# The last pair's second convolution ahead of pair 6's gate, four pieces of the hand-over to the pages in another order, and the last 28 results closer

## The chip, the cores and the metric

The kernel runs on one core of a Trainium2 chip. The metric is the device time of one execution in microseconds; lower is better. A core has TensorE (PE), VectorE (DVE), ScalarE (ACT), GpSimd (POOL) and SyncE (SP), which run their own instruction streams and wait for one another by semaphores. DMA queues are issued from SP, ACT and POOL.

## What is computed

The input x has 16 images of 64 channels and 32x32 points. It goes through a binary convolution block and then, point by point (16384 tokens of 64 values), through a mixture of 16 experts of which each token takes 2:

```
x = x + conv_block(layernorm_over_channels(x))
    # pad, sign, 2x3 convolution with sign(w1), batch norm, relu,
    # pad, sign, 2x3 convolution with sign(w2), batch norm, + input, relu
t = tokens(x)                                  # 16384 x 64
n = layernorm(t)
p = softmax(n @ gate_w + gate_b); top 2 of 16, renormalised
t = t + sum over the 2 experts e of
        p_e * (silu(n @ w1[e]) * (n @ w2[e])) @ w3[e]
```

## The kernel before

**Stage 1, pairs.** Two images make a pair (128 partitions are 2 x 64 channels), so there are pairs 0 to 7. Each goes through centring, root of the variance, first and second convolution, residual, second centring, variance and root, turning of channels (`channels` puts the rows to be sent into `payload`), gate, choice of two experts, and *places*: counts and ranks on TensorE, and `slots` on VectorE, which computes where in a list of pages each token goes. POOL then sends the pair's 16 x 128 rows to that list in memory (`scatter`, L523, 16 indirect DMAs a pair). The steps are software-pipelined in a loop over t: in step t, TensorE works on pair t-1's convolutions, pair t-2's gate (with `b = t - 2`) and pair t-3's ranks. Each engine's program is written out by hand in its own order, and that order is what decides who waits.

**Stage 2, pages.** A page is 128 rows that share a set of four experts (a *line*). There are 147 pages in 37 groups of up to 4. SP loads a group's pages (L408, L409) once their rows are in memory; the order of the pages is computed after pair 3 (`order_pages`, `order_rows`). `order_rows` stands in VectorE's program behind a wait for pair 6's gate, since both use the bank `small`. TensorE turns the rows of a group (`turn_rows`, L857), ScalarE makes a float16 high part (`rows_high`) and VectorE the low part (`rows_low`, L1475). Per page TensorE computes 32 up products (L947, L948) with the four experts that the *roster* names; the offsets are read into TensorE's registers (`experts_of`), so the roster (8 short steps on VectorE, `roster_step`) must be there. ScalarE applies silu (L702), VectorE multiplies (`hide`, L1557), TensorE does the down products (L962), VectorE weighs and sums (L1568, L1578, L1583) and POOL gives each page's results back to memory with an indirect DMA (`give_back`, L511).

Pairs 0 to 3 are known before the first page is loaded; pairs 4 to 7 are still being placed while pages run. From group 10 on (`SOON` is 40 pages), SP loads pages only after the scatters of all eight pairs. Pair 5's places (`weights`, `slots`) are computed in the straight piece between the loop over pairs and the loop over pages. The second choice of pair 6 is made at page 1 and its slots at page 6; those of pair 7 at pages 6 and 11. POOL sends pair 7's rows alternately with the first 16 give-backs, and after that waits before each give-back of page n until `result_page(n)` pages have passed ScalarE (`silu_done`), and for the result itself. Pair 7's scatter order and some waits of POOL on other engines (`let_through`) space the sends: the fifth send of pair 4 asks for `gate_ready` of pair 6.

**The end.** Groups of the last pages are summed in twos (from page 132). When all give-backs have landed, SP loads the last pair's results, TensorE turns them, VectorE adds the input and ScalarE stores.

Of the kernel before, what the change touches and what calls it, by code (L numbers as in the profile page):

```python
# [6 lines left out]
ACT = mybir.ActivationFunctionType  # L7
# [8 lines left out]
P = 128  # L16
# [34 lines left out]
def metaformer_kernel(nc, x, w1, gamma1, beta1, mean1, var1, w2, gamma2, beta2, mean2, var2,  # L51
# [33 lines left out]
    with ExitStack() as ctx:  # L85
# [226 lines left out]
        def pages_of(g):  # L312
            return min(BY, PAGES - BY * g)
# [127 lines left out]
        def _(pool):  # L441
# [59 lines left out]
            def result_page(n):  # L501
                last = PAGES - 20
                return max(17 + 3 * n // 4, min(n, last) + 9 + 3 * max(n - last, 0) // 4)
# [33 lines left out]
        def _(act):  # L537
# [107 lines left out]
            def make_hi(m):  # L645
                act.wait_ge(weights_made, WM_SCALES)
                act.activation(up_w[m][:, :, :], up_raw[:, m, :, :], ACT.Copy, scale=scales[:, m:m + 1])\
                    .then_inc(hi_made, 1)

            act.wait_ge(dve_made, DM_ZEROS)  # L650
            for t in range(PAIRS + 2):
# [13 lines left out]
                if a < PAIRS:  # L665
                    for c in range(CH):
                        sign(c, a)
                    for c in range(CH):
                        square(c, a)
                    for c in range(CH):  # L670
                        copy(c, a)
                if 0 <= b < PAIRS:
                    channels(b)
# [15 lines left out]

            def rows_high(g):  # L690
                act.wait_ge(rows_turned, g + 1)
                if g >= 2:
                    act.wait_ge(up_ready, BY * (g - 1))
                width = pages_of(g) * P
                act.activation(xs_hi[g % 2][:, 0:width], rows_bank(g)[:, 0:width], ACT.Copy, scale=X_SCALE)\  # L695
                    .then_inc(xs_hi_ready, 1)

            def silu(n):
# [6 lines left out]
            act.preload_act_table_set("silu_and_others")  # L705
            rows_high(0)
            for n in range(PAGES):
# [13 lines left out]
        def _(pe):  # L721
# [142 lines left out]
            for t in range(PAIRS + 2):  # L864
# [23 lines left out]
                if t == PAIRS + 1:  # L888
                    turn_rows(0)
                if 0 <= b < PAIRS:  # L890
                    if b == 0:
                        pe.wait_ge(gate_in, 48)
                    gate(b)
                if 0 <= s < PAIRS:
                    for c in range(CH):
                        conv(1, c, s)
# [112 lines left out]
        def _(dve):  # L1009
# [529 lines left out]

            for k in range(8):  # L1540
                roster_step(0, k)
            weights(PAIRS - 3)
# [3 lines left out]
            newton_root(1, PAIRS - 1)  # L1546
            channels(PAIRS - 1)
            first_choice(PAIRS - 2)
            score(PAIRS - 1)
            rows_low(0)  # L1550

# [98 lines left out]
```

## Time and profile before

| what | value |
|---|---|
| three timed runs | 528.3, 532.3, 535.14 us; median 532.3 |
| profiled execution | 528.8 us, its span 526.8 us |
| mean granted clock of TensorE in it | 0.948 of 2.4 GHz |
| busy share of the span | PE 90%, DVE 75%, ACT 49%, POOL 54% |
| chain that ended last, by engine | PE 64%, DVE 14%, POOL 8%, issue 8%, ACT 3%, DMA 2% |

Times are in microseconds from the start of the span. An instruction's row gives its start, its length, and in brackets how long its engine had been idle before it and what ended that wait. Matmuls overlap, so that a row's length includes some of the next one's. Of a row that ends in xN, N instructions are merged.

### The profile page before, as it was taken

Reading aid. Unit: us, or ns where it says so; the run is one execution under the profiler, and the core shown is the slowest. Engines: PE = TensorE matmul, PEld = TensorE weight load, DVE = VectorE, ACT = ScalarE, POOL = GpSimd, SP = SyncE. Lnnn points to the kernel's source line nnn. Section 1 sums busy time; section 2 is a strip of 40 time slices with the busy share of each in tenths; the row PEclk is TensorE's granted clock in tenths of the full one; section 3 lists DMA queues with packets and bytes.
Section 4 is the critical chain, followed back from the end, with each engine's and each line's share of the span. In section 5 each row is a group of like instructions: output and inputs, shape, how many; then the busy total and the mean of one; then the engine's idle time right before and its main releaser. Section 6 shows DMA issues by size and latency. Waiting matters only on the chain.

```text
span 526.8 us, 15132 instructions
## 1 busy us (share of the span) xinstructions
PE 473.7 (90%) x4774; PEld 416.0 (79%) x4774; DVE 397.1 (75%) x917; ACT 257.0 (49%) x461; POOL 284.2 (54%) x378
## 2 busy tenths in 40 slices
PE   6889989898996858689999999999999999999983
PEld 6557667665774558679998999999999999999982
DVE  5457787988888779888766777777877778777783
ACT  4467788976884543224343443443434434344320
POOL 4000006877777777677777754445444454445652
PEclk9689899998998879789999999999999999999996
DMA  6981011020200343011213332232333524211034
GB/s 263 330 159 42 0 42 55 32 67 28 69 30 29 85 94 81 26 32 43 57 36 80 79 72 52 47 87 56 88 97 87 137 53 127 58 34 54 25 124 160
DMA packets 62664, 41.03 MB, mean 78 GB/s; under 512 B 50003, under 2 KB 54318, under 8 KB 62080
## 3 DMA queue, kind: packets, MB, share of 16 engines
q1 hardware_dynamic: 52208, 23.84, 19.7%
q0 software_dynamic: 8800, 8.94, 5.3%
q10 hardware_dynamic: 1584, 7.29, 3.4%
q8 instruction: 45, 0.74, 0.6%
q14 instruction: 27, 0.22, 0.1%
HBM read 21.46 MB, written 19.19 MB: 77 GB/s over the span
## 4 chain that ended last, share of the span: by engine, by line
PE 64%; DVE 14%; POOL 8%; issue 8%; ACT 3%; DMA 2%; SPq 1%; POOLq 0%; DVEq 0%; ACTq 0%
PE turn L962 21%; PE up L947 10%; PE up L948 10%; PE up L772 8%; POOL pages L523 5%; PE small L789 4%; POOL results L511 3%; PE small L818 3%; PE small L857 2%; PE up L747 2%; PE turn L801 1%; PE lines L969 1%; ACT rstd_wide L587 1%; DVE up_w L1166 1%; PE turn L862 1%
## 5 line engine op out<-in xcount | busy, mean ns | idle before, releaser
L511 POOL DMA_INDIRECT results<-result,page_in x147 | 146.7, 998 | 117.9 <-ACT xc L702 87.1
L523 POOL DMA_INDIRECT pages<-payload,slot_int x128 | 131.4, 1026 | 107.3 <-DVE slot_int L1376 69.5
L702 ACT ACTIVATE xc<-up,gate_unscale 128x512 f32<-128x512 f32 x147 | 101.2, 688 | 179.5 <-PE up L948 157.5
L947 PE MATMUL up<-xs_hi,up_w 128*128 128x128 f16 x1176 | 150.1, 221 | 7.6 <-DVE sq L1557 3.2
L948 PE MATMUL up<-xs_lo,up_w 128*128 128x128 f16 x1176 | 150.1, 221 | 0.0
L947 PEld LDWEIGHTS up<-xs_hi,up_w 128*128 x1176 | 124.1, 106 | 8.4 <-issue 8.3
L948 PEld LDWEIGHTS up<-xs_lo,up_w 128*128 x1176 | 116.6, 99 | 0.1
L1557 DVE SCALAR_TENSOR_TENSOR hidden<-up,hidden_scale,xc 128x512 f32<-128x512 f32 x74 | 55.5, 749 | 37.3 <-ACT xc L702 34.6
L962 PE MATMUL turn<-down_raw,sq 128*128 x584 | 80.2, 281 | 1.6 <-DVE branch L1568 0.4
L962 PE MATMUL turn<-down_raw,hidden 128*128 x592 | 78.1, 275 | 1.4 <-issue 0.4
L962 PEld LDWEIGHTS turn<-down_raw,sq 128*128 128x128 f32 x584 | 71.6, 193 | 9.2 <-issue 6.9
L962 PEld LDWEIGHTS turn<-down_raw,hidden 128*128 128x128 f32 x592 | 72.2, 193 | 6.3 <-issue 5.4
L1557 DVE SCALAR_TENSOR_TENSOR sq<-up,hidden_scale,xc 128x512 f32<-128x512 f32 x73 | 54.5, 747 | 21.2 <-ACT xc L702 19.5
L772 PE MATMUL up<-sign,conv_w 128*128 128x512 bf16 x192 | 53.2, 435 | 0.0
L772 PEld LDWEIGHTS up<-sign,conv_w 128*128 128x128 bf16 x192 | 21.1, 116 | 25.9 <-issue 11.1
L789 PE MATMUL small<-mean_col,sq 128*128 128x2 f32 x256 | 32.4, 257 | 6.1 <-ACT sq L613 3.5
L789 PEld LDWEIGHTS small<-mean_col,sq 128*128 128x128 f32 x256 | 31.8, 201 | 7.2 <-ACT sq L613 4.1
L1568 DVE TENSOR_TENSOR branch<-turn,page_in 128x512 f32<-128x512 f32 (+1 forms) x38 | 25.9, 683 | 6.2 <-PE turn L962 6.1
L1568 DVE TENSOR_TENSOR rstd_wide<-turn,page_in 128x512 f32<-128x512 f32 x36 | 24.8, 689 | 5.8 <-PE turn L962 5.7
L695 ACT ACTIVATE xs_hi<-small 128x512 f16<-128x512 f32 (+1 forms) x36 | 21.4, 594 | 9.7 <-PE small L857 9.6
L1475 DVE SCALAR_TENSOR_TENSOR xs_lo<-small,xs_hi 128x512 f16<-128x512 f32 (+1 forms) x36 | 24.3, 676 | 0.0
L857 PE MATMUL small<-ident,page_in 128*128 128x128 f32 x143 | 22.7, 283 | 0.8 <-DMA page_in<-pages 0.8
(238 smaller groups left out, 598.0 us busy)
## 6 DMA issues: line engine op xcount, KB each, us to landing
pages<-x ACTq DMA_DIRECT2D x4, 1332.0 KB, 10.8
page_in<-pages SPq DMA_DIRECT2D x147, 36.0 KB
page_in<-pages SPq DMA_DIRECT2D x147, 32.0 KB
x_in<-in_x SPq DMA_DIRECT2D x7, 512.0 KB, 3.5
out<-up_raw SPq DMA_DIRECT2D x5, 512.0 KB, 2.9
results<-result,page_in POOLq DMA_INDIRECT x147
up_raw<-in_L_ffn_w SPq DMA_DIRECT2D x4, 512.0 KB, 17.1
pages<-payload,slot_int POOLq DMA_INDIRECT x128, 2.2
```

What stands on the lines that cost most here:

```text
L511: pool.indirect_dma_start(out=results, out_offset=bass.IndirectOffsetOnAxis(ap=page_in[g % LOADS][:, k, D + AT_TOKEN:D + AT_TOKEN + 1].bit ...
L523: pool.indirect_dma_start(out=pages, out_offset=bass.IndirectOffsetOnAxis(ap=slot_int[q % PAYLOADS][:, t:t + 1], axis=0), in_=payload[q % ...
L702: act.activation(act_s[n % 2], up[n % 2][:, 0:CW], ACT.Silu, scale=gate_unscale[:, 0:1])\
L772: last = pe.matmul(cv[c], conv_w[:, which, t, :], image[:, c * ROWS + i:(c + 1) * ROWS + i, j:j + W], start=(t == 0), stop=(t == len(TAPS) ...
L789: last = pe.matmul(var_ps[n][:, 2 * j:2 * j + 2], sq[:, j * P:(j + 1) * P], mean_col[:, :], start=True, stop=True)
L857: last = pe.transpose(rows_bank(g)[:, k * P:(k + 1) * P], page_in[g % LOADS][:, k, 0:2 * D], ident[:, :])
L947: pe.matmul(target, own, xs_hi[g % 2][:, at], start=True, stop=False)
L948: last = pe.matmul(target, own, xs_lo[g % 2][:, at], start=False, stop=True)
L962: last = pe.matmul(target, hidden[n % RING][:, at], whole[:, bass.ds(e, D)], start=True, stop=True)
L1475: dve.scalar_tensor_tensor(out=xs_lo[g % 2][:, 0:width], in0=rows_bank(g)[:, 0:width], scalar=X_SCALE, in1=xs_hi[g % 2][:, 0:width], op0=A ...
L1557: dve.scalar_tensor_tensor(out=hidden[n % RING], in0=up[n % 2][:, CW:HW], scalar=hidden_scale[:, 0:1], in1=act_s[n % 2], op0=ALU.mult, op1 ...
L1568: dve.tensor_tensor(weighed[g % 2][:, k:k + count, :, :], down_pair(m)[:, 0:count, :, :], weights.unsqueeze(3).to_broadcast([P, count, PER ...
```

## The change

Five pieces of code move or change; the instructions are the same in number.

- TensorE, step t = 8 (`PAIRS`): `conv(1, c, 7)`, the second convolution of the last pair, stands before `gate(6)` instead of behind it. The product that turns the page order (L887) stays ahead of both.
- ScalarE, step t = 9: `rows_high(0)` stands before `channels(7)` instead of behind the loop and a table load.
- VectorE, between the loops: weights and slots of pair 5, root and channels of pair 7 and the low rows of group 0 come before the roster, and the score of pair 7 and the first choice of pair 6 come last, in that order.
- POOL: `last` in `result_page` is `PAGES - 28` instead of `PAGES - 20`; pages from 120 on are asked for earlier.

```diff
             def result_page(n):
-                last = PAGES - 20
+                last = PAGES - 28
                 return max(17 + 3 * n // 4, min(n, last) + 9 + 3 * max(n - last, 0) // 4)
...
+                if t == PAIRS + 1:
+                    rows_high(0)
                 if 0 <= b < PAIRS:
                     channels(b)
...
             act.preload_act_table_set("silu_and_others")
-            rows_high(0)
             for n in range(PAGES):
...
                 if t == PAIRS + 1:
                     turn_rows(0)
+                if t == PAIRS:
+                    for c in range(CH):
+                        conv(1, c, s)
                 if 0 <= b < PAIRS:
                     if b == 0:
                         pe.wait_ge(gate_in, 48)
                     gate(b)
-                if 0 <= s < PAIRS:
+                if 0 <= s < PAIRS - 1:
                     for c in range(CH):
                         conv(1, c, s)
...
-            for k in range(8):
-                roster_step(0, k)
             weights(PAIRS - 3)
             slots(PAIRS - 3)
             newton_slack(1, PAIRS - 1)
             newton_sum(1, PAIRS - 1)
             newton_root(1, PAIRS - 1)
             channels(PAIRS - 1)
+            rows_low(0)
+            for k in range(8):
+                roster_step(0, k)
+            score(PAIRS - 1)
             first_choice(PAIRS - 2)
-            score(PAIRS - 1)
-            rows_low(0)
```

TensorE in step t = 8, from the turning of pair 6's channels on (`page_at` is the page order, `gate_mat` the gate, `sign` with `conv_w` the convolution), before:

```order
L887 MATMUL small<-ident,page_at 2x128
L818 MATMUL small<-gate_mat,xc 128x32 x8
L772 MATMUL up<-sign,conv_w 128x512 x12
L827 MATMUL lines<-ident_b,chosen 128x128 x2
L835 MATMUL lines<-incident,chosen_t 128x160 x2
L758 MATMUL up<-x,center_mat 128x256 x4
L841 MATMUL lines<-line_hot,upper_b 128x340
```

and with the change:

```order
L888 MATMUL small<-ident,page_at 2x128
L773 MATMUL up<-sign,conv_w 128x512 x12
L819 MATMUL small<-gate_mat,xc 128x32 x8
L828 MATMUL lines<-ident_b,chosen 128x128 x2
L836 MATMUL lines<-incident,chosen_t 128x160 x2
L759 MATMUL up<-x,center_mat 128x256 x4
L842 MATMUL lines<-line_hot,upper_b 128x340
```

The twelve products of the convolution stand ahead of the eight of the gate; line numbers are one higher in the changed file.

VectorE between the loops, from pair 7's channels (`payload`) on: first choice of pair 6 (from `best` to `logits<-pick`), score of pair 7 (`logits<-small` and the next), low rows (`xs_lo`), first `hide`; before:

```order
L1227 TENSOR_TENSOR payload<-turn,rstd 128x8x64
L1258 TENSOR_REDUCE best<-logits 128x16
L1236 TENSOR_TENSOR match<-logits,best 128x256
L1239 TENSOR_TENSOR key<-match,first_rank 128x256
L1242 TENSOR_REDUCE best<-key 128x16
L1244 TENSOR_TENSOR pick<-key,best 128x256
L1265 SCALAR_TENSOR_TENSOR logits<-pick,logits 128x256
L1250 TENSOR_TENSOR logits<-small,rstd 128x256
L1253 TENSOR_TENSOR logits<-logits,gate_bias 128x256
L1475 SCALAR_TENSOR_TENSOR xs_lo<-up,xs_hi 128x512
```

and with the change, where the eight roster steps go from `reached` to the cast of `roster`:

```order
L1231 TENSOR_TENSOR payload<-turn,rstd 128x8x64
L1479 SCALAR_TENSOR_TENSOR xs_lo<-up,xs_hi 128x512
L1451 TENSOR_TENSOR reached<-page_at,opened 128x322
L1454 TENSOR_REDUCE total_reached<-reached 128x2
L1456 TENSOR_REDUCE pairs_behind<-reached 128x2
L1460 SCALAR_TENSOR_TENSOR line_of<-pairs_behind,total_reached 128x2
L1463 TENSOR_TENSOR on_page<-line_of,line_number 128x40
L1467 TENSOR_TENSOR expert_on_page<-on_page,expert_of 128x80 x2
L1471 TENSOR_REDUCE roster_f<-expert_on_page 128x8
L1473 CAST roster<-roster_f 128x8
L1254 TENSOR_TENSOR logits<-small,rstd 128x256
L1257 TENSOR_TENSOR logits<-logits,gate_bias 128x256
```

The low rows now follow channels at once, the roster follows them, and the score and the first choice, whose rows come next, stand behind it.

## Rows read from the trace of the kernel before

**Rows 1.** Waits of TensorE, 190 to 285 us: engine, line, releaser: us, times, longest.
```profile
PE small L857 <- DMA page_in<-pages: 0.8, 1, 0.8
```

**Rows 2.** Chain of waits: start us, us, what.
```profile
278.87 1.91 DMA page_in<-pages
```

**Rows 3.** Timeline of POOL: start us, us, engine, line, operation, tiles [idle before <-releaser].
```profile
173.98 0.96 POOL L523 DMA_INDIRECT pages<-payload,slot_int  x1 [0.30 <-issue]
...
212.29 0.96 POOL L523 DMA_INDIRECT pages<-payload,slot_int  x1 [2.11 <-DVE slot_int L1376]
```

**Rows 4.** Timeline of VectorE, 170 to 194 us.
```profile
170.47 0.28 DVE L1432 CAST order<-small 2x128 int32<-2x128 f32 x1 [0.83 <-PE small L818]
...
173.03 0.75 DVE L1190 SCALAR_TENSOR_TENSOR bn_sum<-up,bn,x_ln 128x512 f32<-128x512 f32 x1 [0.83 <-PE up L772]
...
175.34 0.75 DVE L1190 SCALAR_TENSOR_TENSOR bn_sum<-up,bn,x_ln 128x512 f32<-128x512 f32 x1 [1.56 <-PE up L772]
...
176.48 1.35 DVE L1197 TENSOR_TENSOR x<-x_in,bn_sum 128x512 f32<-128x512 f32 x2 [0.39 <-ACT bn_sum L604]
...
178.97 0.49 DVE L1447 TENSOR_TENSOR reached<-page_at,opened 128x322 f32<-128x322 f32 x1
...
181.94 0.17 DVE L1336 TENSOR_SCALAR rounded_up<-lines 128x20 f32<-128x20 f32 x1
...
185.98 0.19 DVE L1376 CAST slot_int<-slot 128x16 uint32<-128x16 f32 x1
...
187.37 0.41 DVE L1258 TENSOR_REDUCE best<-logits 128x16 f32<-128x256 f32 x1
...
190.79 0.68 DVE L1475 SCALAR_TENSOR_TENSOR xs_lo<-up,xs_hi 128x512 f16<-128x512 f32 x1
...
193.54 0.75 DVE L1557 SCALAR_TENSOR_TENSOR hidden<-up,hidden_scale,xc 128x512 f32<-128x512 f32 x1 [2.07 <-PE up L948]
```

**Rows 5.** Timeline of TensorE, 167 to 192 us.
```profile
167.40 0.27 PE L887 MATMUL small<-ident,page_at 128*2 128x128 f32 x1 [4.55 <-DVE slack L1213]
...
167.51 2.92 PE L818 MATMUL small<-gate_mat,xc 128*128 128x32 f32 x16
...
170.24 5.06 PE L772 MATMUL up<-sign,conv_w 128*128 128x512 bf16 x12
...
177.37 1.97 PE L758 MATMUL up<-x,center_mat 128*128 128x256 f32 x8 [1.17 <-DVE x L1197]
...
179.46 1.34 PE L845 MATMUL lines<-line_hot,ones_b 128*128 128x320 bf16 x16
...
183.35 0.60 PE L857 MATMUL up<-ident,page_in 128*128 128x128 f32 x4
...
186.52 1.97 PE L818 MATMUL small<-gate_mat,xc 128*128 128x32 f32 x16 [2.56 <-DVE slack L1213]
...
191.61 0.29 PE L947 MATMUL up<-xs_hi,up_w 128*128 128x128 f16 x1 [3.12 <-DVE xs_lo L1475]
```

**Rows 6.** Stretches: us, PE, PEld, DVE, ACT, POOL busy (instructions), clock, DMA share, GB/s.
```profile
171.00:172.50 1.50, 1.50 (x5) 0.58 (x4) 1.16 (x4) 0.00 (x0) 1.10 (x2) 0.50 0.08 27
...
192.00:193.50 1.50, 1.50 (x16) 1.50 (x14) 0.00 (x0) 0.69 (x1) 1.13 (x2) 0.50 0.41 87
```

**Rows 7.** Timeline of SP's DMA issues.
```profile
174.91 0.38 SPq L409 DMA_DIRECT2D page_in<-pages  x1
```

**Rows 8.** Timeline of ScalarE.
```profile
189.82 0.60 ACT L695 ACTIVATE xs_hi<-up 128x512 f16<-128x512 f32 x1
```

**Rows 9.** Timeline of POOL near the end.
```profile
510.98 0.98 POOL L511 DMA_INDIRECT results<-result,page_in  x1 [1.47 <-DVE result L1583]
```

**Rows 10.** Stretch 450 to 500 us, columns as in Rows 6.
```profile
450.00:500.00 50.00, 49.48 (x614) 47.13 (x614) 37.90 (x61) 20.11 (x31) 26.00 (x27) 1.00 0.17 43
```

**Rows 11.** VectorE's sum: 280 to 300 us, then 440 to 488; busy, mean ns, idle.
```profile
L1578 DVE TENSOR_TENSOR halves<-rstd_wide 128x512 f32<-128x512 f32 x1 | 0.7, 692 | 0.0
...
L1578 DVE TENSOR_TENSOR halves<-rstd_wide 128x512 f32<-128x512 f32 x3 | 2.1, 692 | 0.1
```

More of the change, by code:

```diff
@@ L648, in make_hi, with rows_high @@
                     .then_inc(hi_made, 1)
+            def rows_high(g):
+                act.wait_ge(rows_turned, g + 1)
+                if g >= 2:
+                    act.wait_ge(up_ready, BY * (g - 1))
+                width = pages_of(g) * P
+                act.activation(xs_hi[g % 2][:, 0:width], rows_bank(g)[:, 0:width], ACT.Copy, scale=X_SCALE)\
+                    .then_inc(xs_hi_ready, 1)
             act.wait_ge(dve_made, DM_ZEROS)
@@ L688, in _ @@
                     make_hi(0)
[L690 to L696, printed above, removed]
             def silu(n):
```

## The prediction

> **What bounds the kernel now.** I read the page's busy shares first: TensorE is busy 90% of the span, so in the long page stage the end is set by how many pages remain, and a change in front of that stage counts only if it moves the start of it or a stall inside it. The reader is to look for such stalls in TensorE's waits from 190 to 285 us: one wait there is for a page in memory, 0.8 us, at the turning of group 10 [rows 1]. Group 10 is the first group that may hold rows of the last pairs, so SP loads it only after all scatters of pair 7; the chain of waits shows that load at 278.87, 1.91 us long [rows 2]. The chain leads back over an unbroken row of POOL's DMAs (16 scatters of pair 6, then 16 of pair 7 with 16 give-backs between them) to 212.29, where POOL had stood idle for 2.11 us until pair 6's slots were cast [rows 3]. So two paths meet at 280 us, 0.8 us apart: TensorE's own pages, and the path over pair 6's slots and POOL. Whatever moves VectorE's work at the start of the page stage moves the second path one for one, since VectorE goes from its first product of `hide` (193.54, [rows 4]) to pair 6's slots almost without idling. That first `hide` is the number that I follow.
>
> **Part 1: the last convolution ahead of pair 6's gate, on TensorE.** The product that turns the page order stands ahead of both and waits 4.55 us for VectorE, until 167.40 [rows 5]. The convolution does not pass it, so it does not fill that gap; it only trades places with the gate. Gate: 167.51 to 170.24, 2.73 us. Convolution: 170.24 and 5.06 us as printed, or about 4.90 from start to start [rows 5]. Both ran at half clock (granted 0.50, the level of 1.2 GHz, [rows 6]) after that gap, which stays as it was, so I keep both lengths. Then the gate ends at about 167.51 + 4.90 + 2.73 = 175.14 where it ended at 170.24: 4.9 us later. Next I ask who waits for it. VectorE's next instruction in program order is the copy of the page order (170.47, 0.23 us behind the gate, [rows 4]); it waits for the gate, and the add-ins of the convolution's result are queued behind it. From that copy to the point where VectorE was free for the add-ins took 173.03 - 0.83 - 170.47 = 1.73 us. After the change: copy at 175.37, free at 177.10, add-ins at 177.10 and 177.76, residual 1.14 us behind the second one (176.48 - 175.34) at 178.90. It was at 176.48, so **+2.4 us**: the convolution's result lies ready and nobody takes it.
>
> Centring of pair 7 (177.37) and the ranks of pair 5, whose last product ends at 179.46 + 1.34 = 180.80 [rows 5], stand behind that residual on TensorE and go with it: ranks ready at 183.2. Others behind the gate: the copy of the order also releases SP's page loads. Group 0's last load was issued at 174.91 [rows 7]; 4.9 later and with 1.91 us to landing it is there at 181.7, and group 0 is turned at 183.35 + 2.4 = 185.75 [rows 5], so about 4 us of cover remain. POOL's fifth scatter of pair 4 (173.98, [rows 3]) asks for the same gate and stalls about 1.4 us; the 2.11 us of idleness before pair 6 hides that.
>
> **Part 2: the order of VectorE's last steps ahead of the pages.** Before: roster, weights and slots of pair 5, root and channels of pair 7, first choice of pair 6, score of pair 7, low rows. The roster with the weights took 181.94 - 178.97 = 2.97 us [rows 4], of it about 0.4 for the two weight instructions (my estimate from their size), so the roster 2.6. Slots 5 are now free of it and wait for the ranks: they start at 183.2 in place of 181.94, **+1.3 us**, where without part 1 they could start at about 181.0, 0.9 earlier. From there: slots cast 185.98 + 1.3 = 187.3; root and channels 187.37 - 185.98 = 1.39, to 188.7; the low rows now follow at once, 0.6 of VectorE's time, to 189.3 (before: 190.79). The high rows that they need took 0.60 us on ScalarE at 189.82 [rows 8], behind channels; now they stand ahead of them and run from about 186.4, so they are hidden, at no cost. The eight roster steps end at 189.3 + 2.6 = 191.9. TensorE waits for rows and roster, and reads the four offsets of its first page only then; before, that reading lay in the wait of 3.12 us for the low rows. I have no row for its length; between 0.2 and 0.9 us it puts the first page product at 192.1 to 192.8 (it was 191.61, [rows 5]). Score and first choice, 190.79 - 187.37 = 3.42 us [rows 4], now lie behind the roster: VectorE is free at 191.9 + 3.4 = 195.3. The product that `hide` needs is 193.54 - 191.61 = 1.93 us behind the first page product, at 194.0 to 194.7, so VectorE is the later one whatever the reading costs. First `hide` at 195.3 where it was 193.54: **+1.8 us**. The 2.07 us that VectorE idled there are used up by the 3.4 us put in, which is why taking work off the way to the low rows brings nothing.
>
> **Part 3: the last 28 results closer.** `result_page` holds a give-back until a later page has passed ScalarE, and is now closer for pages 120 to about 138. At the end POOL is not behind: it idled 1.47 us for VectorE's result at 510.98 [rows 9], and the last five follow one another whatever went before. **0 us.**
>
> Sum: 528.8 us (the profiled execution, span 526.8) + 1.8 + 0 = 530.6. That execution is at the low end of what was seen; the mean of it and the three timed runs (528.3, 532.3, 535.14) is 531.1, their median alone 532.3. I add the 1.8 to 531.1: **532.9 us**, 0.3% slower, which no measurement of this kernel can tell from nothing: about 2% is what one can tell.
>
> **Rivals.**
> 1. *The trade costs nothing on the way to pair 5's slots* (chance 0.20). If the convolution's early result reaches the residual in the old time, say since the pair runs faster than the half clock of [rows 6] once the wide products come first, the ranks are ready at 181.0, the first `hide` comes at 193.0 (0.9 + 3.4 as above against 193.54), and the sum is -0.5: 530.6 from the mean. Against it: VectorE's queue cannot reach the add-ins before the gate.
> 2. *The clock* (0.20, slower side). After the wait of 3.12 us the first pages still ran at 0.50 at 193.5 [rows 6], so from 191.61 at least 1.9 us of products went at half clock, a loss of 1.0. The slow stretch at the convolution covered about 7.8 us of products (167.51 to 170.24 + 5.06, [rows 5]). If the second one falls as fully on page products, it costs 3.9 in place of 1.0; with half of that 2.9 hidden behind VectorE, which sets the pace there, that is +1.4 on top of 1.8: 534.3.
> 3. *Group 0 arrives late* (0.05, slower). Decides when its loads take over 4 us longer than 1.91; each us beyond delays all pages. At 3 us beyond, 535.9.
> 4. *POOL closer to VectorE's sums* (0.03, slower). If a give-back and a sum exclude each other, seven sums of two instructions meet a POOL instruction of 0.98 us [rows 9]: up to 13.7 us, of which VectorE's idleness there (50 - 37.9 us in 50, [rows 10]) takes 9.7 over 40 us; +4.0, 536.9. Against it: the same sum lasts 692 ns where POOL works without a break and 692 ns where it works half the time [rows 11].
>
> [...]
>
> The forecast itself has 0.50; 0.02 is left for what I do not see.
>
> **Numbers.** The cases reach from 530.6 to 536.9 around a mean of 531.1, while single runs of the same kernel lay 2.8 below and 4.0 above that mean. The low end is case 1 in a low run (528.3 - 0.5 = 527.8, rounded to 528.0), the high end the clock case at 534.3 with most of the upper spread: 537.5. All cases but the last lie inside 2%: faster 0.02, same 0.95, slower 0.03.
>
> **What the new profile would show.** The gate of pair 6 behind the twelve wide products, ending near 175; the copy of the order right behind it and both add-ins with no idle time; the residual near 178.9; slots of pair 5 cast near 187.3; xs_lo of group 0 ahead of the roster, near 188.7; the first `hide` near 195.3 with no idle time before it; POOL idle for about 2.4 us before pair 6 (2.11 + 1.8 - 1.4); TensorE's wait at group 10 still near 0.8. I am wrong if the residual is not later than 176.5, if the first `hide` comes by 193.5, or if POOL's way to group 10 opens before pair 6's slots.

## The result, and the profile after

| | before | with the change |
|---|---|---|
| 20 runs each, median | 530.91 us (526.18 to 539.82) | 535.79 us (531.81 to 543.11) |
| ratio of after to before, 95% interval | | **1.0088 [1.0056, 1.0119]** |
| profiled execution | 528.8 us, span 526.8 | span 535.2 us |
| granted clock, mean | 0.948 | 0.921 |

The change makes the kernel slower by about 4.7 us (0.88%). I had forecast 0.3%, 532.9 us in a range of 528.0 to 537.5: the sign and the places were right, the size was a little over a third of the measured one. The interval does not hold 1, though I had written that such a difference could not be told from nothing. The same kernel against itself (r1 below) gave 1.0041 [0.9979, 1.0104].

The spans of the two profiles differ by 8.4 us, and that is not the cost of the change. The product that turns the page order, ahead of which TensorE's instructions are the same, starts at 167.40 us before [rows 5] and at 171.78 after. These 4.4 us come from where stretches of half clock fall in stage 1 (last section). So I count everything from that product, in every profile, and call it the *anchor*. (The ratios leave out single runs more than 1.5% above the fastest of the same kernel; the profiled executions of e1, e10 and r1 were such runs, and r1 shows that up to pair 6's slots the piece behind the anchor is none the longer for it.)

TensorE with the change (timeline: start us, length, engine, line, operation, tiles, idle time before and its releaser):

```profile
171.78 0.37 PE L888 MATMUL small<-ident,page_at 128*2 128x128 f32 x1 [4.25 <-DVE slack L1217]
...
171.94 5.32 PE L773 MATMUL up<-sign,conv_w 128*128 128x512 bf16 x12
...
177.06 1.97 PE L819 MATMUL small<-gate_mat,xc 128*128 128x32 f32 x16
...
183.08 3.75 PE L759 MATMUL up<-x,center_mat 128*128 128x256 f32 x8 [3.15 <-DVE x L1201]
...
187.19 1.51 PE L846 MATMUL lines<-line_hot,ones_b 128*128 128x320 bf16 x16
...
198.44 0.28 PE L951 MATMUL up<-xs_hi,up_w 128*128 128x128 f16 x1 [2.00 <-DVE roster L1473]
```

The convolution is ahead of the gate and took 5.1 us from start to start, the gate ends near 178.9, and centring (L759) finds nobody's residual: TensorE idles 3.15 us. To be seen behind it: centring takes 3.75 us for the eight products that took 1.97 before [rows 5], and the ranks come late in turn. The granted clock in 183 to 188 was 0.55, as the stretches of the same profile show (columns as in Rows 6):

```profile
183.00:188.00 5.00, 4.92 (x16) 3.60 (x17) 2.04 (x7) 3.12 (x6) 3.98 (x4) 0.55 0.46 96
...
205.00:207.00 2.00, 0.99 (x15) 0.85 (x16) 2.00 (x4) 0.59 (x3) 1.59 (x2) 1.00 0.52 108
...
209.00:211.00 2.00, 2.00 (x20) 2.00 (x21) 1.93 (x5) 0.64 (x1) 1.65 (x2) 0.50 0.29 75
```

The other two rows matter further on: at 209 to 211, in the middle of the first pages, it is at 0.50 again. VectorE, same profile:

```profile
179.07 0.28 DVE L1436 CAST order<-small 2x128 int32<-2x128 f32 x1 [5.05 <-PE small L819]
...
180.71 1.40 DVE L1194 SCALAR_TENSOR_TENSOR bn_sum<-up,bn,x_ln 128x512 f32<-128x512 f32 x2
...
182.24 1.35 DVE L1201 TENSOR_TENSOR x<-x_in,bn_sum 128x512 f32<-128x512 f32 x2
...
188.74 0.18 DVE L1340 TENSOR_SCALAR rounded_up<-lines 128x20 f32<-128x20 f32 x1 [3.49 <-PE lines L846]
...
192.92 0.31 DVE L1380 CAST slot_int<-slot 128x16 uint32<-128x16 f32 x1
...
194.38 0.68 DVE L1479 SCALAR_TENSOR_TENSOR xs_lo<-up,xs_hi 128x512 f16<-128x512 f32 x1
...
197.44 0.17 DVE L1473 CAST roster<-roster_f 128x8 int32<-128x8 f32 x1
...
201.06 0.74 DVE L1561 SCALAR_TENSOR_TENSOR hidden<-up,hidden_scale,xc 128x512 f32<-128x512 f32 x1
...
219.96 0.17 DVE L1380 CAST slot_int<-slot 128x16 uint32<-128x16 f32 x1
```

Order copy behind 5.05 us of idleness, add-ins and residual in one unbroken row at 182.24, which is 10.46 us behind the anchor (before 9.08); slots of pair 5 start 16.96 behind it (14.54) and wait 3.49 us for the ranks; low rows ahead of the roster; first `hide` at 201.06, 29.28 behind the anchor (26.14 before), without idling, as forecast. And the slots of pair 6 are cast at 219.96, which is 48.18 behind the anchor. Before, that row was

```profile
211.31 0.17 DVE L1376 CAST slot_int<-slot 128x16 uint32<-128x16 f32 x1
```

43.91 behind it. So 4.27 us are lost up to there: 3.14 ahead of the first `hide`, 1.13 behind it. From the slots of pair 6 to the end it is 315.24 us after and 315.49 before, the same within 0.3. What POOL waited for ahead of pair 6's first scatter:

```profile
220.94 0.96 POOL L523 DMA_INDIRECT pages<-payload,slot_int  x1 [5.79 <-DVE slot_int L1380]
```

It idled 5.79 us before pair 6's first scatter, where it had idled 2.11 in the kernel before [rows 3] (3.28 and 3.39 in two other profiles with this piece unchanged, e3 and r1). TensorE's wait at group 10, forecast near 0.8 us, was

```profile
289.04 0.66 PE L858 MATMUL small<-ident,page_in 128*128 128x128 f32 x4 [0.18 <-DMA page_in<-pages]
```

0.18 us, because TensorE's own pages had become as late as the load: it turned group 9 at 104.33 us behind the anchor before and at 108.72 after. Group 0 was turned without a wait for its pages.

### The profile page after: what moved, and what is told of

The parts are those of the page before. It is cut to its first block, busy times and chain, and to the rows that moved or that the text cites. A ratio compares the mean times of both kernels' runs of the same rounds, so it can differ in the third digit from the quotient of the medians.

```text
span 535.2 us, 15132 instructions
## 1 busy us (share of the span) xinstructions
PE 483.1 (90%) x4774; PEld 421.7 (79%) x4774; DVE 397.7 (74%) x917; ACT 257.4 (48%) x461; POOL 281.2 (53%) x378
## 3 DMA queue, kind: packets, MB, share of 16 engines
q10 hardware_dynamic: 1584, 7.29, 3.4%
## 4 chain that ended last, share of the span: by engine, by line
PE 69%; DVE 8%; POOL 8%; issue 7%; ACT 4%; DMA 2%; SPq 1%; ACTq 0%; POOLq 0%; DVEq 0%
PE turn L966 21%; PE up L773 10%; PE up L951 10%; PE up L952 9%; PE small L790 5%; POOL pages L523 5%; POOL results L511 3%; PE small L858 2%; PE small L819 2%; PE up L748 2%; PE turn L802 2%; PE up L759 1%; PE lines L846 1%; PE lines L973 1%; PE turn L813 1%
## 5 line engine op out<-in xcount | busy, mean ns | idle before, releaser
L523 POOL DMA_INDIRECT pages<-payload,slot_int x128 | 129.2, 1010 | 118.8 <-DVE slot_int L1380 76.9
L773 PE MATMUL up<-sign,conv_w 128*128 128x512 bf16 x192 | 57.2, 459 | 0.0
```

What stands on the lines that cost most here:

```text
L523: pool.indirect_dma_start(out=pages, out_offset=bass.IndirectOffsetOnAxis(ap=slot_int[q % PAYLOADS][:, t:t + 1], axis=0), in_=payload[q % ...
L773: last = pe.matmul(cv[c], conv_w[:, which, t, :], image[:, c * ROWS + i:(c + 1) * ROWS + i, j:j + W], start=(t == 0), stop=(t == len(TAPS) ...
```

## The experiments

All profiles in one table, in us. "Anchor" is the start of the product that turns the page order; the other columns are counted from it. "To the end" is the span less the anchor.

| kernel | anchor | residual of 7 | first hide | slots of 6 cast | to the end | time against before |
|---|---|---|---|---|---|---|
| before | 167.40 | 9.08 | 26.14 | 43.91 | 359.4 | |
| before, again (r1) | 175.61 | 8.84 | 25.99 | 43.76 | 360.2 | 1.0041 [0.9979, 1.0104] |
| the change | 171.78 | 10.46 | 29.28 | 48.18 | 363.4 | 1.0088 [1.0056, 1.0119] |
| the change, again (r2) | 174.92 | 9.26 | 27.40 | 47.83 | 364.1 | 1.0115 [1.0032, 1.0198] |
| e1 order of VectorE and tail only | 178.33 | 8.91 | 25.34 | 45.17 | 361.2 | 1.0040 [1.0000, 1.0081] |
| e2 convolution only | 167.64 | 9.47 | 27.49 | 45.12 | 362.0 | 1.0061 [1.0013, 1.0108] |
| e3 tail only | 171.43 | 9.08 | 26.21 | 43.88 | 359.4 | 0.9986 [0.9933, 1.0040] |
| e4 convolution in the gap | 171.66 | 5.34 | 24.30 | 41.99 | 358.5 | 0.9977 [0.9930, 1.0024] |
| e4, again (r4) | 174.12 | 5.36 | 23.10 | 40.78 | 357.5 | 0.9969 [0.9920, 1.0018] |
| e6 change, add-ins first | 176.71 | 7.23 | 24.48 | 42.10 | 359.4 | 1.0146 [1.0062, 1.0229] |
| e7 change, wait filled | 167.93 | 9.47 | 25.89 | 45.64 | 361.7 | 1.0134 [1.0067, 1.0201] |
| e9 gap, choice in the wait | 174.80 | 5.36 | 23.65 | 41.33 | 357.8 | 535.44 against 532.49 us, no ratio |
| e10 change, pages filled | 176.94 | 9.27 | 27.36 | 45.01 | 361.9 | 1.0008 [0.9952, 1.0063] |
| r3 gap, add-ins first | 173.92 | 3.73 | 22.56 | 40.23 | 357.4 | 0.9968 [0.9916, 1.0019] |

How steady the column is: the three profiles in which nothing of this piece is changed (before, r1, e3) give 43.91, 43.76 and 43.88 us to the slots of pair 6 and 359.4, 360.2 and 359.4 to the end, though their anchors lie 8 us apart. A single run's time spreads by 13 us; the pieces behind the anchor are what tells kernels apart here. Two other kernels were profiled twice and agree less well: the change differs from its repeat by 0.35 us at the slots and 0.7 at the end, e4 from its repeat by 1.21 and 1.0. A difference of about 1 us between single profiles is therefore not safe.

**e1, the order of VectorE and the tail alone** (convolution back behind the gate).

```diff
-                if t == PAIRS:
-                    for c in range(CH):
-                        conv(1, c, s)
                 if 0 <= b < PAIRS:
...
-                if 0 <= s < PAIRS - 1:
+                if 0 <= s < PAIRS:
```

> The changed kernel with the last convolution back behind pair 6's gate: VectorE's and ScalarE's new order and the closer last results stay. I measure from the product that turns the page order on TensorE to VectorE's first product of hide: 26.1 us before (167.40 to 193.54), 29.3 us with the whole change (171.78 to 201.06). Theory A (the convolution's place costs, because VectorE's add-ins stand in its queue behind the wait for the gate): 25.6 us, half a microsecond better than before, time 0.998 to 1.001 of before. Theory B (the new order on VectorE costs: 3.4 us of score and first choice now between roster and first hide): about 28 us and time 1.005 or more.

First hide 25.34 behind the anchor: theory A to within 0.3 us, B falls for the part ahead of the pages. But the slots of pair 6 are 45.17 behind it, not 43.3, and the time is 1.0040. The loss lies behind the first `hide`, where neither theory had it. TensorE's anchor and VectorE's rows in e1:

```profile
178.33 0.37 PE L888 MATMUL small<-ident,page_at 128*2 128x128 f32 x1 [3.61 <-DVE slack L1214]
```

```profile
203.67 0.74 DVE L1558 SCALAR_TENSOR_TENSOR hidden<-up,hidden_scale,xc 128x512 f32<-128x512 f32 x1
...
216.19 0.69 DVE L1569 TENSOR_TENSOR branch<-turn,page_in 128x512 f32<-128x512 f32 x1 [1.23 <-PE turn L963]
...
223.50 0.17 DVE L1377 CAST slot_int<-slot 128x16 uint32<-128x16 f32 x1
```

From first `hide` to slots it takes 19.83 us where it took 17.77 before. Inside it `weigh` (second row) waits 1.23 us for TensorE, which it did not in the kernel before. This was my first surprise, and e10 is made for it.

**e2, the convolution alone.**

```diff
+                if t == PAIRS:
+                    for c in range(CH):
+                        conv(1, c, s)
                 if 0 <= b < PAIRS:
...
-                if 0 <= s < PAIRS:
+                if 0 <= s < PAIRS - 1:
```

> The kernel before with nothing but the last convolution ahead of pair 6's gate (behind the product that turns the page order). Theory A: the residual of pair 7 starts about 2.4 us later counted from that product (9.1 us behind it before, 11.5 now), TensorE then idles about 3 us for it, and the first hide comes at 28.5 us or more from the product; time 1.004 to 1.010. Theory B: as before, 26.1 us, time within 0.2%.

```profile
167.64 0.27 PE L887 MATMUL small<-ident,page_at 128*2 128x128 f32 x1 [4.54 <-DVE slack L1216]
...
177.95 3.75 PE L758 MATMUL up<-x,center_mat 128*128 128x256 f32 x8 [3.15 <-DVE x L1200]
```

Theory A in direction: TensorE's wait for the residual is 3.15 us (1.17 before) and centring is at half rate. The sizes are smaller than expected: residual at 9.47 in place of 11.5, since in this profile the granted clock fell later, so that the convolution ran in 4.28 us and the gate in about 1.8. First hide 1.35 later, slots of pair 6 1.21 later, 2.3 us to the end (mean of the three profiles with this piece unchanged: 359.7), ratio 1.0061. Theory B's "as before" falls. From 22 to 114 us behind the anchor the mean granted clock is 0.87 (0.90 and 0.91 in the two profiles of before), and TensorE turns group 10 without a wait for its pages, 115.68 us behind the anchor (113.42 and 114.29): here TensorE's own pages are the later path.

**e3, the last 28 results closer, alone.**

```diff
-                last = PAGES - 20
+                last = PAGES - 28
```

> The kernel before with nothing but the last 28 results closer. Theory A (POOL is not behind at the end, it waits for VectorE's results): the last five give-backs follow as before, the end unchanged, time 0.998 to 1.002. Theory C (POOL beside VectorE's sums slows them, one port pair held by one of the two): the sums of 128x512 in the last 40 us take longer than 692 ns and the time is 1.003 or more.

```profile
507.09 0.98 POOL L511 DMA_INDIRECT results<-result,page_in  x1 [1.60 <-DVE result L1583]
...
514.98 0.98 POOL L511 DMA_INDIRECT results<-result,page_in  x1 [1.50 <-DVE result L1583]
```

POOL waits for VectorE's result 1.60 and 1.50 us before the last give-backs, as it waited 1.47 in [rows 9]; 0.9986 and 359.4 us to the end. Nothing, as forecast. The sums in its last stretch:

```profile
L1578 DVE TENSOR_TENSOR halves<-branch 128x512 f32<-128x512 f32 x2 | 1.4, 692 | 0.1
```

692 ns, no more than in [rows 11]: C falls.

**e4, the convolution in the gap**, one place further forward than in the change.

```diff
                 if t == PAIRS:
+                    for c in range(CH):
+                        conv(1, c, s)
                     pe.wait_ge(order_link, 18)
...
-                if 0 <= s < PAIRS:
+                if 0 <= s < PAIRS - 1:
```

> The kernel before with the last convolution one place further forward than in the change, ahead of the product that turns the page order, so that it falls into TensorE's wait of 4.5 us. Theory A: it runs at full clock in 2.7 us, the gate keeps its time or ends earlier, the add-ins find their result ready behind an order copy that is not late, the residual starts 2 to 4 us earlier, and the first hide comes at 22.5 to 24 us from the product that turns the order; time 0.992 to 0.997 of before. Theory B says nothing here; a theory by which the residual is not what paces this piece (D: the root of pair 7 or the page loads do) expects 26 us and no change.

```profile
171.66 0.27 PE L889 MATMUL small<-ident,page_at 128*2 128x128 f32 x1 [0.76 <-DVE slack L1215]
...
177.83 3.75 PE L758 MATMUL up<-x,center_mat 128*128 128x256 f32 x8 [3.16 <-DVE x L1199]
```

The wait ahead of the anchor is 0.76 us in place of 4.55 and the residual comes at 5.34, 3.7 earlier; theory D falls, the residual paces this piece. First hide 24.30, 1.8 us better. Half of the early residual is lost in the hand-over: TensorE still idles 3.16 us for it, now because the gate ends earlier too, and centring again runs at half rate. To the end 358.5 us; ratio 0.9977, whose interval holds 1.

**e6, the add-ins ahead of the wait for the gate**, on the changed kernel.

```diff
                     if t == PAIRS:
+                        for c in range(CH):
+                            conv2(c, s)
+                        for c in range(CH):
+                            residual(c, s)
                         dve.wait_ge(gate_ready, b + 1)
                         order_rows()
...
-                if 0 <= s < PAIRS:
+                if 0 <= s < PAIRS - 1:
                     for c in range(CH):
                         conv2(c, s)
```

> The changed kernel, and on VectorE the add-ins and residual of pair 7 now stand ahead of the wait for pair 6's gate. Theory A (the queue behind that wait is what made the traded convolution a loss): the residual starts at about 7 us behind the product that turns the page order (10.5 with the change, 9.1 before), although the order copy stays at about 7.3 or later; TensorE's wait for the residual shrinks from 3.15 us to under 1. The first hide then comes at 26 us or a little less in place of 29.3, and the time falls to about before, ratio 1.000 to 1.005. A theory by which the late order copy (page loads) makes the loss expects 29 us still.

```profile
176.71 0.37 PE L888 MATMUL small<-ident,page_at 128*2 128x128 f32 x1 [3.67 <-DVE slack L1217]
...
184.78 1.96 PE L759 MATMUL up<-x,center_mat 128*128 128x256 f32 x8 [1.11 <-DVE x L1201]
...
192.79 0.66 PE L858 MATMUL up<-ident,page_in 128*128 128x128 f32 x4 [1.10 <-DMA page_in<-pages]
```

This is the test of the step by which I had forecast a loss, and it holds: with the convolution still traded, residual at 7.23 in place of 10.46 or 9.26, TensorE's wait 1.11 in place of 3.15, centring at full rate, first hide at 24.48 (27.40 and 29.28), although the order copy is later than ever (8.45). The late copy now costs something else: TensorE waits 1.10 us for group 0's pages (third row). It turns them 3.4 us earlier than with the change (16.08 against 19.47 behind the anchor) and the copy is 1.2 later, which uses up the 4 us of cover that I had estimated. To the end it is 359.4, as before the change. The timed ratio, 1.0146 from four runs, says the opposite. The profile is of the run of 537.84 us, whose length lies ahead of the anchor (176.71); the other three runs have no profile. So e6 shows the effect of the queue in the piece, and not in the time.

**e7, TensorE's wait filled**, on the changed kernel; the extra products go to a bank that centring overwrites.

```diff
+                if q == PAIRS - 1 and c == 0:
+                    for k in range(14):
+                        pe.matmul(cen[0], conv_w[:, 1, 0, :], sign2[:, 0:ROWS, 0:W], start=True, stop=True)
                 pe.wait_ge(x2_ready, CH * q + c + 1)
```

> The changed kernel with 14 extra 128x512 products (their result is overwritten) on TensorE where it waits 3.15 us for pair 7's residual: it is no longer idle there. Theory A with the clock (the idle time let the granted clock fall to 1.2 GHz, so that centring and the first ranks ran at half rate): centring takes 1.97 us in place of 3.75, pair 5's slots start 1.3 to 1.8 us earlier (15.3 in place of 16.96 behind the product that turns the order), the first hide at 27.5 to 28 in place of 29.3, the time 0.2 to 0.4% better than the changed kernel. Without a role of the clock: everything at its old place or later by what the extra products exceed the wait.

```profile
167.93 0.37 PE L891 MATMUL small<-ident,page_at 128*2 128x128 f32 x1 [3.52 <-DVE slack L1220]
...
174.92 3.19 PE L758 MATMUL up<-sign,conv_w 128*128 128x512 bf16 x14
...
178.14 1.99 PE L762 MATMUL up<-x,center_mat 128*128 128x256 f32 x8
```

Centring 1.99 us in place of 3.75 or 3.51: the half rate came of the idle time. The other profiles agree: behind waits of 3.15 to 3.33 us (both of the change, e2, e4 and its repeat, e9, e10) and of 1.70 (r3) centring ran at half rate, behind waits of 1.11 to 1.17 (before, r1, e1, e3, e6) at full rate. The slots of pair 5 start at 13.71 (16.96 and 15.11), the first hide is at 25.89, more than expected. To the end 361.7, 2 us less than the changed kernel. Again the time of four runs (1.0134), of which one is profiled, does not show it.

**e10, the early pages filled**, on the changed kernel.

```diff
+                if n == 3:
+                    pe.wait_ge(channels_ready[0], PAIRS)
+                    for k in range(5):
+                        pe.matmul(turn[0][:, :], conv_w[:, 1, 0, :], sign2[:, 0:ROWS, 0:W], start=True, stop=True)
                 if n in TURN:
                     turn_chosen(TURN[n])
+                if n == 3:
+                    for k in range(5):
+                        pe.matmul(turn[0][:, :], conv_w[:, 1, 0, :], sign2[:, 0:ROWS, 0:W], start=True, stop=True)
```

> The changed kernel with twice five extra 128x512 products (their result is overwritten) at page 3, around the turning of pair 6's choice, where TensorE waits 1.43 and 1.24 us for VectorE. Theory A with the clock (VectorE 1.2 us behind TensorE at the first hide, TensorE idles more there, the clock falls and pages 4 to 5 run at half rate): the half-clock stretch 6 to 9 us behind the first hide is gone, and slots of pair 6 are cast 17.8 us behind the first hide in place of 18.9. If the stretch has nothing to do with that idle time, 18.9 stays, or 19 to 20 by the extra products.

Its first hide is at 204.30. The stretches 4 to 10 us behind it:

```profile
208.00:210.00 2.00, 2.00 (x14) 1.05 (x13) 2.00 (x5) 0.49 (x2) 1.39 (x3) 1.00 0.42 93
...
210.00:212.00 2.00, 1.98 (x28) 1.81 (x25) 1.90 (x5) 0.69 (x1) 1.67 (x2) 1.00 0.32 66
...
212.00:214.00 2.00, 2.00 (x30) 2.00 (x27) 1.93 (x5) 1.17 (x2) 1.42 (x2) 1.00 0.34 80
```

No half clock, where the changed kernel had 0.50 in 209 to 211, 8 us behind its first `hide`. First `hide` to slots of pair 6: 17.65 us, where the changed kernel took 18.90 and 20.43 and e1 19.83. It starts from the same first `hide` as r2 (27.36 and 27.40), and has 2.8 us less at the slots. But e6 has no such stretch either (17.62 us), with nothing filled, so one profile of e10 does not show that the filling did it. To the end 361.9, time 1.0008.

**e9, gap, and the first choice in VectorE's wait for the ranks.**

```diff
+                    for c in range(CH):
+                        conv(1, c, s)
                     pe.wait_ge(order_link, 18)
...
             for k in range(8):
                 roster_step(0, k)
+            first_choice(PAIRS - 2)
             weights(PAIRS - 3)
...
             channels(PAIRS - 1)
-            first_choice(PAIRS - 2)
+            rows_low(0)
             score(PAIRS - 1)
-            rows_low(0)
```

(and `rows_high(0)` ahead of `channels(7)`, as in the change)

> A version meant to beat both: the last convolution ahead of the product that turns the page order; roster first as in the kernel before; first choice of pair 6 behind the roster, where VectorE waits for the ranks of pair 5; then weights and slots 5, root and channels 7, low rows at once (high rows early on ScalarE), score of pair 7 last; results as before. Theory A: residual at 5.3 us, slots of pair 5 at about 13.2, low rows at 19, first page product at 19.7, first hide at 21.6 us (24.3 with the convolution in the gap alone, 26.1 before) with VectorE idle ahead of it, so that no page product waits for VectorE and no half-clock stretch falls on pages 2 to 4; slots of pair 6 at 39 to 40 (43.9 before). Time 0.990 to 0.995 of before, if pair 6's slots and POOL still set the way to group 10; 0.997 if TensorE's early pages already filled the time.

Residual 5.36 and low rows at 19.15 as expected, but the first hide at 23.65, 2 us later: pair 7's gate ran at half rate (3.62 us), and so did the first pages, at 0.50 from 7 us ahead of the first `hide` to 3 behind it. 357.8 us to the end; four runs, with no ratio. It is not shown to beat the plain e4 (358.5 and 357.5).

**r1 and r2, both kernels again.**

> The kernel before, unchanged, for a second profile. In the profiles so far the product that turns the page order starts anywhere from 167.4 to 178.3 us though nothing ahead of it differs; steps of stage 1 take 11.5 or 14.8 us as half-clock stretches fall. Theory A: the piece from that product to pair 6's slots is 43.9 us here too, within 1.5, wherever the product lies; ratio 1.000 within its interval. If the piece itself swings by 3 us or more, the 4.3 us that it grew with the change is not shown by one pair of profiles.

```profile
175.61 0.37 PE L887 MATMUL small<-ident,page_at 128*2 128x128 f32 x1 [3.69 <-DVE slack L1213]
```

```profile
219.37 0.18 DVE L1376 CAST slot_int<-slot 128x16 uint32<-128x16 f32 x1
```

219.37 - 175.61 = 43.76: the piece is as long as in the first profile, with the anchor 8.2 us later.

> The changed kernel, unchanged, for a second profile. Theory A: the piece from the product that turns the page order to pair 6's slots is 2 to 4.5 us longer than in the kernel before (46 to 48.5), the residual 9.3 to 10.5 us behind the product, TensorE idle about 3.15 us for it; ratio 1.005 to 1.010.

```profile
174.92 0.37 PE L888 MATMUL small<-ident,page_at 128*2 128x128 f32 x1 [3.68 <-DVE slack L1217]
...
185.02 3.51 PE L759 MATMUL up<-x,center_mat 128*128 128x256 f32 x8 [3.15 <-DVE x L1201]
```

```profile
202.32 0.74 DVE L1561 SCALAR_TENSOR_TENSOR hidden<-up,hidden_scale,xc 128x512 f32<-128x512 f32 x1
...
222.75 0.17 DVE L1380 CAST slot_int<-slot 128x16 uint32<-128x16 f32 x1
```

47.83 us to the slots. The change costs 4.27 in one pair of profiles and 4.07 in the other, though it falls differently: 1.41 ahead of the first `hide` and 2.66 behind it here, 3.14 and 1.13 in the first. In r2 centring took 3.51 but ranks ran at full rate; in exchange 0.50 fell on the pages.

**r3 and r4, versions that might beat both.** r4 is e4 again; r3 is e4 with the add-ins first, as in e6.

> The last convolution ahead of the product that turns the page order, and VectorE's add-ins and residual of pair 7 ahead of the wait for pair 6's gate; all else as in the kernel before. Theory A: residual 3.5 us behind the product (5.3 with the convolution in the gap alone), order copy at 5 to 6, no wait of TensorE for the residual above 1.5 us, first hide at 22.5 to 23.5 (24.3), slots of pair 6 at 40.3 to 41.2 (42.0; 43.9 before). POOL then is the one that comes last before pair 6's scatter, so that little of it reaches the end: time 0.994 to 0.999 of before.

```profile
173.92 0.27 PE L889 MATMUL small<-ident,page_at 128*2 128x128 f32 x1 [0.21 <-DVE slack L1215]
...
178.49 3.75 PE L758 MATMUL up<-x,center_mat 128*128 128x256 f32 x8 [1.70 <-DVE x L1199]
```

Residual 3.73, order copy 5.00, first hide 22.56, slots of pair 6 40.23, all as expected; TensorE's wait 1.70, and centring all the same at half rate.

> The convolution in the gap alone, once more, as its 0.9977 had an interval that holds 1. Theory A: first hide at 24.3 and slots of pair 6 at 42.0 us behind the product that turns the order, 1.9 us ahead of the kernel before; time 0.995 to 0.999, better than both kernels.

First hide 23.10 and slots 40.78, a little better than e4. Both are 3.1 to 3.6 us ahead of before (43.85) at the slots of pair 6, and 2.2 to 2.3 at the end: 357.4 and 357.5 against 359.7. The medians on one chip were 529.49 and 530.35 against 534.5 for before and 536.98 for the changed kernel. Against before the intervals still hold 1 ([0.9916, 1.0019] and [0.9920, 1.0018]), so that they are faster than before is likely and not settled. They are faster than the changed kernel, whose interval on that chip begins at 1.0032.

## Why the prediction was right, and where its size was off

That 535.8 us lies in the range is partly luck and proves little: I had widened the range by the spread of single runs, so that it would have held any shift of the mean of 531.1 from -3.1 to +6.4 us. What the sum says of each step is the test.

**The traded convolution is a loss, because VectorE's add-ins stand behind the wait for the gate.** Right. The gate ended 4.9 us later by my sum, the order copy came 4.2 later (7.29 against 3.07), the add-ins followed without a pause, and e6, which changes nothing but that queue, takes the loss back up to the first `hide` and, in its profile, to the end. The size was too high: the sum gave +2.4 for the residual; against the mean of the two profiles of before (8.96) it was +1.5 in the first profile and +0.3 in r2: the residual was 3.2 us behind the order copy and not 3.5, and in r2 the order copy itself came at 6.09, the convolution having run partly at full clock. I had kept half clock for both, but behind the convolution the gate took 1.8 us and not 2.73. So the condition of my rival 1, a pair that runs faster than half clock, came true in part, and in r2 nearly in full.

**What follows the residual goes with it, at unchanged lengths.** Wrong in size, the other way. I moved centring and ranks by 2.4 us and kept their 1.97 and 1.34 us. In fact TensorE's wait grew from 1.17 to 3.15 us and what came next ran at half clock: centring alone 3.75. Slots 5 went from 14.54 to 16.96, +2.4 in place of the +1.3 of my sum; in r2 they came at 15.11, +0.7 against r1 (14.38). e7 shows it: with the wait filled centring is 1.99. That the mean of +2.4 and +0.7 is near my +1.3 is luck: a residual sized too high and a centring sized too low partly cancel.

**VectorE sets the first hide, +1.8.** Right in kind: VectorE came to it without idling, with 3.5 us of score and first choice put in behind the roster. Measured +3.1 and +1.4, of which the slots of pair 5 bring +2.4 and +0.7; the new order itself adds 0.7 both times, where my sum had 0.5. The reading of the offsets, for which I had no row, took 0.8 us (roster cast until 197.61, first page product at 198.44). That taking work off the way to the low rows brings only half a microsecond was right as well: e1 has its first `hide` at 25.34, 0.7 ahead of the mean of before, where I had said 0.5.

**From there to pair 6's slots nothing changes.** This step failed: "VectorE goes from its first product of `hide` to pair 6's slots almost without idling". With the new order it idles, +1.1 and +2.7 us. A second half-clock stretch of TensorE falls on the first pages, and VectorE waits for its products and for ScalarE's silu of them (0.62 and 0.57 us in the first profile, 1.65 and 0.73 in r2). That is near my rival 2, the clock on the slower side, to which I gave 0.20 and +1.4 us: the kind fits, only that it is a second stretch and not the first one moved, and the price was 1.1, 2.7, 2.1 (e1) and 2.0 us (e7).

The stretch goes with the new order of VectorE. It is there in four of the five profiles that have this order and nothing put in at page 3 (the change twice, e1, e7; not e6), in none of the seven with the old order (before, r1, e2, e3, e4 and its repeat, r3), nor in e9 or e10. What sets it off is open. It is not simply that TensorE idles longer there. Its waits in the 7 us behind the first `hide`, in r2 (with the stretch; first `hide` 202.32) and in r1 (without; 201.60):

```profile
207.26 0.23 PE L951 MATMUL up<-xs_hi,up_w 128*128 128x128 f16 x1 [1.24 <-DVE hidden L1561]
...
208.87 1.96 PE L966 MATMUL turn<-down_raw,hidden 128*128 x8 [0.49 <-DVE sq L1561]
```

```profile
205.03 0.28 PE L827 MATMUL lines<-ident_b,chosen 128*128 128x128 bf16 x2 [0.75 <-DVE chosen L1290]
...
206.56 0.23 PE L947 MATMUL up<-xs_hi,up_w 128*128 128x128 f16 x1 [1.24 <-DVE hidden L1557]
...
208.01 1.10 PE L962 MATMUL turn<-down_raw,hidden 128*128 x8 [0.34 <-DVE sq L1557]
```

These are 1.7 us with the stretch and 2.3 without it.

**The tail: 0.** Right (e3, 359.4 us to the end).

**The sum.** Counted to the end, e1 alone costs 1.5 us (361.2 against 359.7) and e2 alone 2.3, together 3.8, and the whole change 3.7 and 4.4. At the slots of pair 6 they do not add up: 1.3 and 1.3 alone, 4.3 and 4.0 together. With single profiles that differ by up to 1 us from a repeat, I take from this only that each part costs something. My sum had -0.5 for the first and so 2.3 for the second. The first is the term that was off: +1.5 in place of -0.5, lost from the first `hide` to the slots. The second came out as forecast at the end, but again not by my path: 1.2 shows at the slots, and the rest lies on TensorE's own pages, which in e2 are the later path to group 10.

**The rest of the path** I had as pair 6's slots, POOL, group 10, with TensorE's own pages 0.8 us ahead. What was lost up to the slots was still lost at the end (315.24 against 315.49 us), but both paths were late by the same: TensorE's wait at group 10 was 0.18 us, and 1.68 in r2, against 0.79 and none in the two profiles of before. These runs do not tell which of the two carried the loss. POOL's idleness was forecast at 2.4 (2.11 + 1.8 - 1.4 is in fact 2.5) and was 5.79, by the later slots. In the other direction it is not one to one: r3 wins 3.6 us up to the slots and 2.3 at the end. Rival 3, group 0 too late, did not come with the change; rival 4 fell with e3.

## What to carry to other kernels

Bringing work forward on one engine pays only if the engine that takes its result can reach it: look at what the consumer is waiting for in its own program, and if that is the thing just pushed back, the trade is a loss. A wait of 3 us on TensorE is not only its own length: see at what clock the products behind it run. Where single runs spread by more than the effect, count from an event ahead of which nothing differs, to one behind the change; here that piece agreed to 0.15 us in three profiles while the times spread by 13. Profile each kernel twice all the same: two others differed from their own repeats by 0.35 and 1.21 us.

## What the runs showed of the hardware that was not expected

The anchor lay anywhere from 167.40 to 178.33 us although the engines run the same instructions ahead of it (but for the convolution itself in e4, r3, r4 and e9). The difference is in the granted clock. Stretch 75 to 80 us before, and then with the change:

```profile
75.00:80.00 5.00, 4.59 (x30) 3.16 (x31) 4.86 (x24) 4.33 (x8) 0.00 (x0) 1.00 0.01 2
```

```profile
75.00:80.00 5.00, 5.00 (x17) 2.92 (x18) 4.90 (x22) 2.23 (x4) 0.69 (x1) 0.50 0.00 0
```

At 1.00 the step of stage 1 that lies there took 11.5 us (75.4 to 86.9 between two starts of the variances), at 0.50 it took 14.8 (74.0 to 88.8). In most profiles several such steps are hit, in the first profile of before and in e2 and e7 few: anchors 167.40, 167.64 and 167.93. Ahead of the anchor the mean granted clock was 0.94 in the first profile of before and 0.87 in e1 (anchor 178.33). So up to 11 us, 2% of the span, hang on how the half-clock stretches fall on a program that does not change. The timed runs of before spread by 13.6 us, and the two ends of another 35 runs of it show the same sign: 526.51 us at a mean clock of 0.952, 540.31 at 0.925. The Trainium skill, "TensorE: Matmul & The Clock Gate", in "Part 1: The HAM clock gate", says that the same kernel has different numbers of slow products from run to run, and that for modelling the ramp costs under 1% of a typical kernel's span. The first agrees with the anchors here, 167.40 to 178.33. The second does not hold for this kernel: the stretches come back through the whole of stage 1, and their fall alone makes 2%.

The expectation that a filled wait keeps the clock up was met twice (e7 at centring, e10 at the pages), by products whose results are thrown away; for the pages e6 leaves it open whether the filling was needed. No run here tried them in the kernel before.
